# Layer 0 attention with folded value and output weights; layer 2 attention products on four quarters of the array

## The reference

```
# layer 0: one head of width 256, x [64, 64, 256]
h    = film(rmsnorm(x, norm1_w), cond)             # scale and shift per sequence
q, k, v = h @ q_w + q_b, h @ k_w + k_b, h @ v_w + v_b
att  = softmax(q @ k.T / 16) @ v
x    = x + att @ proj_w + proj_b

# layer 2: 16 heads of width 64
h    = modulate(layernorm(x), shift, scale)
q, k, v = split(h @ W_qkv, 3)                      # no bias, inner width 1024
att  = softmax(q_h @ k_h.T / 8) @ v_h              # for each head h
x    = x + gate * (att @ W_out + b_out)
```

## Time and profile before

| | |
|---|---|
| median of 3 runs | 2303.87 us (2302.4 to 2311.68) |
| the profiled execution | 2299.09 us, its span 2297.3 us |
| PE busy | 2173.8 us, 95% |
| DVE busy | 1344.1 us, 59% |
| ACT busy | 987.8 us, 43% |
| POOL busy | 408.2 us, 18% |
| chain that ended last | PE 76%, DVE 10%, issue 8%, ACT 3%, POOL 2% |

### The profile page before, as it was taken

The page is one execution under the profiler, slowest core; times in us unless marked ns, Lnnn a source line. Parts: engine busy times, 40 slices in busy tenths (PEclk is TensorE's granted clock), DMA queues, the critical chain, the costliest instruction groups (busy, mean ns, idle before and its releaser), DMA issues.

```text
span 2297.3 us, 45179 instructions
## 1 busy us (share of the span) xinstructions
PE 2173.8 (95%) x15856; PEld 1748.1 (76%) x15856; DVE 1344.1 (59%) x2570; ACT 987.8 (43%) x1608; POOL 408.2 (18%) x425
## 2 busy tenths in 40 slices
PE   5888999999999999999999999999799999999998
PEld 4777888777777778777777777777688777877887
DVE  4655656677676565654444453344766677775664
ACT  2443555454444333334333333334344555553443
POOL 1112111332321010111111111111611222220000
PEclk9999999999999999999999999999899999999999
DMA  5000000000000000000000000000000000000000
GB/s 206 9 14 9 11 7 14 8 15 7 14 7 10 19 18 9 18 10 2 6 5 5 0 5 5 5 1 2 15 7 5 12 11 5 9 5 1 23 23 28
DMA packets 17855, 33.30 MB, mean 14 GB/s; under 512 B 1266, under 2 KB 11762, under 8 KB 17138
## 3 DMA queue, kind: packets, MB, share of 16 engines
q1 hardware_dynamic: 17778, 32.25, 4.3%
HBM read 28.06 MB, written 4.19 MB: 14 GB/s over the span
## 4 chain that ended last, share of the span: by engine, by line
PE 76%; DVE 10%; issue 8%; ACT 3%; POOL 2%; DVEq 1%; DMA 0%; ACTq 0%; SPq 0%; POOLq 0%
PE psum L502 20%; PE psum L503 18%; PE psum L504 18%; PE psum L592 3%; PE psum L637 3%; PE psum L601 3%; PE psum L582 2%; PE psum L621 2%; PE psum L690 2%; PE psum L538 2%; DVE h_lo L980 1%; DVE xn L961 1%; PE psum L459 1%; DVE hm L971 1%; DVE pb L1029 1%
## 5 line engine op out<-in xcount | busy, mean ns | idle before, releaser
L502 PE MATMUL psum<-h_hi,w_lo 128*128 128x512 f32 x1152 | 485.0, 421 | 34.8 <-DVE h_lo L980 23.2
L503 PE MATMUL psum<-h_lo,w_hi 128*128 128x512 f32 x1152 | 457.0, 397 | 0.0
L504 PE MATMUL psum<-h_hi,w_hi 128*128 128x512 f32 x1152 | 456.8, 397 | 0.0
L1085 DVE TENSOR_TENSOR hid_lo<-hid,hid_hi 128x512 fp32r<-128x512 f32 x256 | 201.6, 788 | 266.1 <-ACT hid_hi L847 265.9
L502 PEld LDWEIGHTS psum<-h_hi,w_lo 128*128 128x128 f32 x1152 | 218.3, 190 | 94.4 <-issue 29.2
L847 ACT ACTIVATE hid_hi<-hid 128x512 fp32r<-128x512 f32 x256 | 161.8, 632 | 226.0 <-PE psum L504 135.4
L504 PEld LDWEIGHTS psum<-h_hi,w_hi 128*128 128x128 f32 x1152 | 217.8, 189 | 53.6
L503 PEld LDWEIGHTS psum<-h_lo,w_hi 128*128 128x128 f32 x1152 | 218.7, 190 | 39.6
L842 ACT ACTIVATE hid<-psum,vec 128x512 f32<-128x512 f32 x192 | 131.9, 687 | 203.4 <-PE psum L504 202.2
L502 PE MATMUL psum<-hid_hi,w_lo 128*128 128x512 f32 x512 | 203.2, 397 | 6.1 <-DVE hid_lo L1085 3.5
L503 PE MATMUL psum<-hid_lo,w_hi 128*128 128x512 f32 x512 | 201.6, 394 | 0.0
(11 more groups left out here) (117 smaller groups left out, 3921.8 us busy)
## 6 DMA issues: line engine op xcount, KB each, us to landing
stage<-in_w_dram SPq DMA_DIRECT2D x24, 256.0 KB, 2.7
stage<-in_w_dram SPq DMA_DIRECT2D x8, 512.0 KB, 3.6
out_dram<-xres SPq DMA_DIRECT2D x8, 512.0 KB, 2.9
xres<-in_x_dram SPq DMA_DIRECT2D x1, 3584.0 KB, 19.3
modw_mod<-in_modw_dram SPq DMA_DIRECT2D x2, 1536.0 KB, 13.8
stage<-in_w_dram SPq DMA_DIRECT2D x8, 384.0 KB, 3.3
stage<-in_w_dram SPq DMA_DIRECT2D x8, 192.0 KB, 2.4
modw_film<-in_modw_dram SPq DMA_DIRECT2D x1, 1024.0 KB, 7.2
```

Source lines behind the costliest of these rows:

```text
L502: nc.tensor.matmul(dst, s_lo, m_hi, start=start and j == 0, stop=False)
L503: nc.tensor.matmul(dst, s_hi, m_lo, start=False, stop=False)
L504: ins = nc.tensor.matmul(dst, s_hi, m_hi, start=False, stop=stop and j == len(pairs) - 1)
L1085: nc.vector.tensor_tensor(hid_lo[:, slot, :], hid32[:, slot, :], hid_hi[:, slot, :].bitcast(F32), ALU.subtract).then_inc(sem["hid"], 1)
```

## The change

- **Layer 0, weights.** v_w and proj_w are multiplied at the start (`fold_vo`: PE transposes v_w, ACT copies, PE multiplies by proj_w, ACT and DVE split the product into its high and low part), and so are the biases (`vo_bias`). The stage `v` then makes h times the folded product; `pv` multiplies by the probabilities and gives rows in the layout of x, in `wide`. The stage `proj`, the transposes of `back`, and the ACT and DVE work on `at_hi`, `at_lo` and `y` are gone from layer 0. POOL adds `vo_bias` to `xres` in `share`.
- **Layer 0, buffers and engines.** `h` alternates between `h_hi`/`h_lo` and `at_hi`/`at_lo`, and `v` between two buffers. `norm` is done by ACT (four instructions), the shift in `turn` by POOL. The exponential is a stage of its own, `exp`. The loop of this phase is written out for all blocks.
- **Layer 0, order.** `q` and `k` belong to the own block; `v` comes last before `exp`.
- **Layer 2.** `pv` and `pv2` are one stage of 16 products. Scores and heads of a pair now lie in halves of two banks, one bank for each half of the array's rows, and the products of each go through all four quarters (rows 0 to 63 or 64 to 127, columns 0 to 63 or 64 to 127) in turn. The transposed probabilities go into the ring `acc_a`. The order of the stages is another.
- **Tables.** The last `table` stages stand after `scores` and `v` of the last block.

```diff
     if layer == 0:
-        return [prev("probs_t"), nxt("stats"), own("scores"), prev("pv"), nxt("norm"), own("v", 0), own("v", 1),
-                nxt("turn"), nxt("split"), prev("proj"), nxt("q", 0), nxt("q", 1), prev("back"), nxt("k", 0),
-                nxt("k", 1), own("divide"), own("share")]
+        return [prev("divide"), own("q", 0), nxt("stats"), own("q", 1), own("k", 0), prev("probs_t"), nxt("norm"), own("k", 1),
+                nxt("turn"), prev("pv"), prev("back"), nxt("split"), own("scores"), own("v", 0), own("v", 1), own("exp"),
+                own("share")]
...
     for p in range(2, PAIRS):
-        body += [own("divide", p - 1), own("scores", p)]
+        body += [own("divide", p - 1), own("scores", p), own("pv", p - 2)]
         if p < 7:
-            body += [own("q", p + 1), own("pv", p - 2), own("k", p + 1)] + ([nxt("turn")] if p == 6 else [])
-            body += [own("pv2", p - 2), own("probs_t", p - 1)]
+            body += [own("q", p + 1)] + ([own("proj", p - 3)] if p >= 3 else [])
+            body += [own("probs_t", p - 1), own("k", p + 1)]
         else:
-            body += [own("pv", 5), nxt("q", 0), own("pv2", 5), nxt("k", 0), own("probs_t", 6)]
-        body += {3: [nxt("stats")], 4: [nxt("norm")], 6: [nxt("split")]}.get(p, [])
-        body += [own("proj", p - 3)] if p >= 3 else []
+            body += [own("proj", p - 3), own("probs_t", p - 1), nxt("q", 0), nxt("k", 0)]
+        body += {3: [nxt("stats")], 4: [nxt("norm")], 5: [nxt("turn")], 6: [nxt("split")]}.get(p, [])
     return body
...
-TABLE_AFTER = [("pv", 0), ("v", 0), ("v", 1), ("proj", 0), ("back", 0), ("share", 0)]
+TABLE_AFTER = [("q", 0), ("k", 0), ("pv", 0), ("scores", 0), ("v", 0), ("v", 1)]
...
                     elif layer == 2:
                         pe.wait_ge(sem["q"], n_at("q", ph, b, k + 1))
-                        wait_alone(pe, sem["k"], n_at("k", ph, b, k + 1))
-                        for g in range(SEQ):
-                            tok = slice(g * S, (g + 1) * S)
+                        pe.wait_ge(sem["k"], n_at("k", ph, b, k + 1))
+                        wait_alone(pe, sem[f"s_free{1 - slot}"], n_at(f"s_free{1 - slot}", ph, b, (k + 1) // 2))
+                        for t in range(TILES):
                             for hd in range(2):
-                                rows = slice(hd * S, (hd + 1) * S)
-                                ins = nc.tensor.matmul(dst[rows, tok], q2_sb[rows, slot, tok], k2_sb[rows, slot, tok],
-                                                       start=True, stop=True)
+                                for g in range(2):
+                                    rows, seq = slice(hd * S, (hd + 1) * S), 4 * (t // 2) + 2 * g + t % 2
+                                    tok = slice(seq * S, (seq + 1) * S)
+                                    ins = nc.tensor.matmul(pair_scores(slot)[g * S:(g + 1) * S, hd, t * S:(t + 1) * S],
+                                                           q2_sb[rows, slot, tok], k2_sb[rows, slot, tok],
+                                                           start=True, stop=True)
...
+            def fold_vo():
+
+                pe.wait_ge(wv_t_done, 1)
+                pe.wait_ge(vo_cols, 2)
+                for m in range(DC):
+                    for kc in range(DC):
+                        nc.tensor.matmul(psum[:, W_BANK, m * D:(m + 1) * D], wv_t[:, kc, m * P:(m + 1) * P], wo[:, kc, :],
+                                         start=kc == 0, stop=kc == DC - 1)
...
-                    for m in range(DC):
-                        for t in range(TILES):
-                            ins = nc.tensor.matmul(wide[:, m, t * P:(t + 1) * P], v0_sb[:, t, m * P:(m + 1) * P],
-                                                   pt[:, 0, t * P:(t + 1) * P], start=True, stop=True)
+                    for t in range(TILES):
+                        ins = nc.tensor.matmul(wide[:, t // 2, (t % 2) * D:(t % 2 + 1) * D], pt[:, 0, t * P:(t + 1) * P],
+                                               v0_sb[b % 2][:, t, :], start=True, stop=True)
                     ins.then_inc(sem["w_full"], 1)
...
+                if s == "norm" and act_norms(ph):
+                    act.wait_ge(sem["rstd"], n_at("rstd", ph, b, 1))
+                    for t in range(TILES):
+                        ins = nc.scalar.activation(xn[:, t, :], xres[:, b * TILES + t, :], ACT.Copy, scale=rstd[:, t:t + 1])
+                    ins.then_inc(sem["normed"], 1)
...
+                    if ph == 0:
+                        if is_first(b):
+                            pool.wait_ge(vo_cols, 3)
+                        pool.wait_ge(sem["normed"], n_at("normed", ph, b, 1))
+                        xs = xres[:, bass.ds(b * TILES, TILES), :]
+                        nc.gpsimd.tensor_tensor(xs, xs, vo_bias[:, :].unsqueeze(1).to_broadcast([P, TILES, D]),
+                                                ALU.add).then_inc(sem["biased"], 1)
```

More of the change, by code:

```diff
@@ L132 @@
 TABLE_BANKS = (3, 5)
-UP_AFTER = {0: [("pv", 0), ("proj", 0)], 1: [("merge", 0), ("proj", 0)],
+UP_AFTER = {0: [("probs_t", 0), ("pv", 0)], 1: [("merge", 0), ("proj", 0)],
             2: [("probs_t", 7), ("proj", 7)], 3: [("merge", 0), ("proj", 0)]}
-W0_PARTS = 4
-def fills_of(kind, layer):
-    body = order_of(kind, layer)
-    fills = [("turn", 0), ("turn", 1)]
-    for off in (1, 0, -1):
-        for s, k, o in body:
-            if o == off and s in ("q", "k", "v"):
-                fills += [(s, k)] * (2 if layer == 1 and s != "v" else 1)
-    return fills
+QK0 = 2 * D
@@ L150, in counts_of, with fills_in, h_readers @@
+def fills_in(kind, layer, s):
+    if s == "turn":
+        return DC
+    if kind == "attn" and s in ("q", "k", "v"):
+        return 2 if layer == 1 and s != "v" else 1
+    return 1 if kind == "attn" and layer == 2 and s == "probs_t" else 0
+def h_readers(kind, layer):
+    body = order_of(kind, layer)
+    return [(s, k) for off in (1, 0) for s, k, o in body if o == off and s in ("q", "k", "v")]
 def counts_of(kind, layer):
@@ L176, in counts_of @@
     if layer == 2:
-        c.update(q=n, k=n, v=8, pv1=n, o_full=n, o_free=n, att_hi=n, att=n, proj=n, w_full=1)
+        c.update(q=n, k=n, v=8, o_full=n, o_free=n, att_hi=n, att=n, proj=n, w_full=1)
     return c
 NAMES = sorted({name for ph in PHASES for name in counts_of(*ph)})
+RING = [f"a_{what}{bank}" for what in ("full", "free") for bank in range(2)]
 def build(nc, x_in, cond_in, mask_k_in, mask_q_in, vec_in, modw_in, weights_in, out, phases=len(PHASES)):
@@ L801, in stage_of @@
                                              scale=SCORE_SCALE[layer]).then_inc(sem["probs"], 1)
+                elif s == "probs_t" and layer == 2:
+                    bank, at = a_slot(ph, s, k, b)
+                    act.wait_ge(sem[f"a_full{bank}"], at + 1)
+                    act.wait_ge(sem["o_full"], n_at("o_full", ph, b, k - 1))
+                    nc.scalar.activation(pt[:, slot, :], acc_a[bank], ACT.Copy).then_inc(sem["probs_t"], 1)
+                    act.wait_ge(sem["probs_t"], n_at("probs_t", ph, b, k + 1))
+                    act.sem_inc(sem[f"a_free{bank}"], 1)
                 elif s == "probs_t":
```

362 lines of the change are left out of this document (226 added, 136 removed).

## The result

The changed kernel takes 2248.62 us (median of 4 runs, 2247.12 to 2249.49) against 2303.14 of the kernel before: a ratio of 0.9754, interval 0.9731 to 0.9778. Its profiled execution has 2249.49 us, 49.6 less than the one of before.

What follows compares the result with a forecast made beforehand. PE, 95% busy, was taken as the bound, with a chain of waits setting layer 0's new turn. From 2299.1 us, −32 for layer 0 and −28 for layer 2 gave 2239, or 2243 as median; range 2208 to 2280.

Steps and rivals of the forecast that it cites:

- Layer 2, the saving per pair: Layer 2 scores and values as one four-quarter group: 1.27 us instead of 2.87, saving PE 1.6 per pair, 12.8 per turn.
- the prediction's own sign: Layer 2: the forecast is wrong if PE's work per turn doesn't fall by 12 us.
- Layer 2, the new waits: Layer 2: PE waits 0.8 us for the `k` copy in six rounds, plus other waits, 10.4 per turn in all.
- the rival of smaller waits: Layer 2: new waits a quarter smaller, making layer 2 −49 us and the time 2222; chance 0.06.
- Layer 0, the chain: Layer 0: the chain from transposes through `h_lo`, scores, exponential, statistics and norm sets a turn of 15.9 against 20.25 us.
- The bias: Layer 0: POOL's `vo_bias` addition, 2 × 1.045 us, lies beside other work; uncovered, it would cost 2.1 per block.
- The clock: Layer 0: PE's gathered wait drops the clock to half, costing 13 us over eight blocks, time 2256; chance 0.11.
- granted clock 1.00 in the turn: Layer 0: sign of the forecast that the clock stays at its full 2.4 GHz during a turn.
- The ends of layer 0: Layer 0: the first block gains nothing; the last gains 6 us, with PE waiting about 5 for the last `divide`.
- Attention 1: Attention 1, among the phases outside layers 0 and 2, was said not to be touched.
- No fourth quarter: Layer 2: more than two quarters don't raise the rate, a group takes 2.2 us, time 2285; chance 0.11.
- quarters that exclude each other: Layer 2: quarters sharing rows or columns can't work together, records go singly, time 2360 to about 2420; chance 0.04.

Runs made afterwards that it cites:

- the two runs on the order of quarters: Changed kernel with layer 2's small products reordered: two array quarters taking turns, 2269.51 us; one quarter after another, 2312.86 us.
- The run with `k` early: Changed kernel with layer 2's next-pair `k` product moved right behind `q`, ahead of `proj` and `probs_t`, in rounds of pairs 2 to 6: 2225.74 us.
- The filler: Changed kernel with eight unread PE products added before PE waits for the next block's norm in layer 0: 2243.68 us.
- no bias: Changed kernel without POOL's addition of the folded bias to x in layer 0, so the result lacks those biases: 2237.81 us.
- `split` first: Changed kernel with the next block's `split` moved ahead of the previous block's `back` in layer 0: 2250.18 us.

## Why the prediction was right

The forecast was 2243, the range 2208 to 2280, and 2248.6 came. Against the profiled execution the sum said −60, and −49.6 came. The two medians were not equally far from their profiled executions, +4.0 before and −0.9 after, which brought back 5 of the 10 us missed, by luck.

- **Layer 2, the saving per pair.** Right in kind, shown by the two runs on the order of quarters. From its first record to the next large product the group took 1.18 us, where the prediction gave 1.27 with some 0.1 of it ahead of the first record. PE's busy time fell by 10.0 per turn where 12.8 was said, so by the prediction's own sign, a fall of at least 12, this term failed. Part of that is bookkeeping: a matmul's row is 0.39 long and its slot 0.23, so each of the six waits that now stand behind a large product (before, one) hides 0.16 in the row ahead, 0.8 more in all. The rest is open.
- **Layer 2, the new waits.** 0.87 us for the copy of k where 0.8 was said, but in five places, not six, as the next block's transposes cover one. For `k` 3 0.50 in place of 1.3, and in the last two rounds 1.30 and 1.22 in place of 1.1 and 2.0. In all 7.98 came in place of 10.4, as the rival of smaller waits had it, and idle time rose by 6.6 in place of 9.1. The two terms missed by nearly the same amount, 2.8 of work and 2.5 of waits, and that −3.39 per turn came so near to −3.5 is luck; in all it is −25.5 against −28. The run with `k` early took away four of the five waits for the copy of k.
- **Layer 0, the chain.** POOL's additions (2.04), the norm on ACT (1.70), what is waited for and once per turn: as said. In turns at full clock even the sum came out, 15.95 against 15.9, but by errors that cancel. `h_lo` was mis-sized, 1.3 for 3.30, since the duration was taken from a turn in which POOL was idle beside it; it ended at 7.5 where 5.9 was said. Three terms went the other way: the copy of v (0.6) was over before the exponential's turn came; from sum to `rstd` 5.2 was said where 4.5 came, and the DVE instruction of 0.88 in the earlier trace rows takes 0.16 now that POOL's split isn't beside it; and the terms as written, 13.95 and 1.7, give 15.65, so that 0.25 of the 15.9 had no row. The bias was priced as work hidden by idle POOL; its price was that DVE waited for it, 0.9 us a turn.
- **The clock.** This rival came true together with the forecast. It was priced at 1.65 per block, and cost 1.2 in three of the six turns between blocks 1 and 7 and 0.6 in one; a fifth drop lies in the turn of block 7. The filler takes them away. The sign "granted clock 1.00 in the turn" held in the early turns alone. The step that failed is the likeliest case, which took a wait of 2 us as harmless. The rows gave 3.37 on one side and 1.3 on the other, and it was closer to the first than the chance of 0.11 said.
- **The ends of layer 0.** −4 where −6 was said, but divided otherwise. The first turn, which was to gain nothing, brought the start of block 1 forward by 5.0 us. The turns from block 1 to block 7 gave 21.7 where 26 was said. The last block with what follows, up to the MLP's second `turn`, took 69.1 us in place of 68.1, so it lost 1.0 where a gain of 6 was said. The step that failed there left the clock out: the two stretches at 0.50 shown above have PE busy for 7.35 us, 3.7 of which full clock would save (an estimate, half of the busy time; no run fills these waits). The wait of PE for the last `divide` was forecast near 5 us and is 4.16, but for another reason: the tables make 0.95 of it, and the exponential behind the copy of v and the load of ACT's table the rest. No run took this apart; it is read from the rows above.
- **Attention 1** was said to be unchanged, and took 1.9 us more. Its turns are 38.8 us or, where the clock drops once, 40.4; one of them was so before and two after; in the runs there are from one (no bias) to five (`split` first). What decides where the drops fall is open.
- **No fourth quarter, and quarters that exclude each other,** fell: with four in turn, records start 15 ns apart on average within a half, not 29 or 58. The Trainium skill, TensorE: Matmul & The Clock Gate, section "Wait — 56ns, not 53.3ns?", states a floor of about 25 ns for the distance between two starts; taken for each record, as the prediction took it, this could not be. The measurement decides: the first four records of the group at 1242.81 start within 0.02 us, one on each quarter, so the floor doesn't hold from one quarter to the next. Counted by products, of two records each, the mean distance is 31 ns, which is no breach of it.

## What to carry to other kernels

Small products on parts of the array are worth interleaving over all quarters in the order in which they are issued; with one quarter after the other, the same buffers and the same single group brought nothing. When a step leaves an engine that is busy for one that idles, ask what shares the time beside it, and take its duration from a row in which both worked. A product placed directly before its reader costs the copy in between; put another stage there before looking for anything larger.

## What the runs showed of the hardware

- From the first to the last start of 64 records of 64 by 64 products it takes 1.04 us in turn over four quarters (16 ns each), 1.48 over the two of a column half in turn (23), and 2.44 with one quarter after the other (39); on one quarter records start 58 ns apart. A product can start before an earlier one for a busy quarter (values at 1193.10, the last scores at 1193.21 and 1193.26, with one quarter after the other).
- DVE's subtraction `h_lo`, with both inputs in SBUF, and POOL's instructions beside it wait for each other: 3.64 us for two subtractions that take 1.29 alone, and 2.83 for an addition that takes 2.35, with 3.64 for all three. DVE's addition in `back`, which reads PSUM, takes 1.22 with POOL's addition beside it, as long as without.
- In the changed kernel six turns of layer 0 begin with a wait of PE of 1.93 to 2.08 us. In five of them the granted clock is 0.50 for 3.4 us behind it; in the one from 51.47 it stays at 1.00. With the wait filled it stayed at 1.00 in all.
